# Attention stage of an audio tower: two of the six value slots multiplied ahead of the spreading of the maxima

## The reference, cut to what matters

```python
attn_grass = einsum('bhnd,bhmd->bhnm', qgr, kgr) ** 2 * grassman_scale   # qgr, kgr from QR
dots = einsum('bhnd,bhmd->bhnm', q, k)
a = concatenate([dots * scale, dots ** 2 * riem_scale, attn_grass], axis=1)
a = (a - bn_mean) * inv + bn_beta
a = einsum('oc,bcnm->bonm', conv_w, a) + conv_b
a = softmax(a, axis=-1)
out = einsum('bhnm,bhmd->bhnd', a, v)
```

## Time and profile before

| what | us |
|---|---|
| median of 3 runs (lowest to highest) | 908.42 (908.27 to 909.32) |
| the profiled execution's own time | 910.35 |
| span of the profiled execution | 908.7 |
| PE matmul busy | 798.0 (88%) |
| DVE busy | 719.1 (79%) |
| POOL busy | 506.5 (56%) |
| ACT busy | 439.6 (48%) |

### The profile page before, as it was taken

The page is one execution under the profiler, slowest core; times in us unless marked ns, Lnnn a source line. Parts: engine busy times, 40 slices in busy tenths (PEclk is TensorE's granted clock), DMA queues, the critical chain, the costliest instruction groups (busy, mean ns, idle before and its releaser), DMA issues. The chain is left out here.

```text
span 908.7 us, 39105 instructions
## 1 busy us (share of the span) xinstructions
PE 798.0 (88%) x16294; PEld 564.3 (62%) x16294; DVE 719.1 (79%) x1291; ACT 439.6 (48%) x902; POOL 506.5 (56%) x551
## 2 busy tenths in 40 slices
PE   3577857899896599999999999999999998799994
PEld 2233325555544477877778777777777776366663
DVE  4488895488798589999899998999998997376772
ACT  2233332211192165655555655555655555277773
POOL 3256571111000578888888888888888885122220
PEclk9578887799998599999999999999999999599998
DMA  8767200022330122222221122222222220001111
GB/s 289 273 212 248 84 1 0 9 54 54 81 88 1 53 70 62 63 62 67 76 63 62 62 65 72 69 62 63 62 64 76 66 62 22 1 18 29 29 28 33
DMA packets 64289, 64.85 MB, mean 71 GB/s; under 512 B 36825, under 2 KB 54812, under 8 KB 64156
## 3 DMA queue, kind: packets, MB, share of 16 engines
q1 hardware_dynamic: 63628, 61.24, 21.8%
q10 hardware_dynamic: 528, 1.54, 0.5%
HBM read 52.93 MB, written 6.75 MB: 66 GB/s over the span
## 5 line engine op out<-in xcount | busy, mean ns | idle before, releaser
L1169 ACT ACTIVATE sq<-ps_dot 128x376 f32<-128x376 f32 x384 | 165.0, 482 | 148.4 <-PE ps_dot L1066 148.4
L1066 PE MATMUL ps_dot<-q_st,k_blk 64*64 64x94 f32 x6144 | 170.5, 249 | 1.0 <-ACT sq L1169 0.8
L1066 PEld LDWEIGHTS ps_dot<-q_st,k_blk 64*64 64x64 f32 x6144 | 134.6, 134 | 46.5 <-issue 28.8
L999 POOL TENSOR_TENSOR v_blk<-v_rep,vmask 128x384 f32<-128x384 f32 x128 | 106.6, 853 | 12.9 <-PE ps_m L1096 7.3
L1014 POOL TENSOR_TENSOR half<-prob 128x564 f32<-128x564 f32 x64 | 75.5, 1180 | 60.5 <-ACT prob L1164 60.5
L1021 POOL TENSOR_TENSOR k_blk<-k_cm,hmask 128x768 f32<-128x768 f32 x64 | 96.8, 1513 | 1.1 <-PE ps_a L1108 1.1
L1023 POOL TENSOR_TENSOR k_mix<-k_cm,cols 128x768 f32<-128x768 f32 x64 | 96.8, 1513 | 0.0
L1192 DVE TENSOR_REDUCE row_max<-ps_a 128x94 f32<-128x564 f32 x128 | 88.8, 736 | 3.6 <-PE ps_a L1116 3.5
L367 PE MATMUL ps_spread<-parts,pair_sel 128*128 128x376 bf16 x256 | 58.1, 369 | 34.5 <-DVE prod L477 22.8
L1116 PE MATMUL ps_a<-sq,mix_w 64*32 64x282 f32 x2048 | 82.6, 404 | 0.3 <-ACT sq L1169 0.3
L1161 ACT ACTIVATE prob<-prob,head_const 128x564 f32<-128x564 f32 x64 | 49.1, 768 | 67.0 <-DVE prob L1214 67.0
(11 more groups left out here) (228 smaller groups left out, 1525.3 us busy)
## 6 DMA issues: line engine op xcount, KB each, us to landing
v_rep<-v_rows SPq DMA_DIRECT2D x128, 192.0 KB, 3.0
x_g<-in_x_dram SPq DMA_DIRECT2D x15, 1500.0 KB, 6.6
v_rows<-tok SPq DMA_DIRECT2D x16, 192.0 KB
q_st<-q_cm SPq DMA_DIRECT2D x64, 47.0 KB, 1.8
out_dram<-rows SPq DMA_DIRECT2D x16, 188.0 KB
x_g<-in_x_dram ACTq DMA_DIRECT2D x1, 1500.0 KB, 7.7
top_rows<-tok SPq DMA_DIRECT2D x16, 32.0 KB
top<-top_rows SPq DMA_DIRECT2D x1, 512.0 KB, 3.4
```

The costliest lines, as they stand in the source:

```text
L999: vb = pool.tensor_tensor(v_blk[:, a, b].rearrange("p t (o d) -> p (t o) d", o=H), v_rep[:, a, b].rearrange("p (t o d) -> p (t o) d", o=H, ...
L1066: mm = pe.matmul(ps_dot[64 * v:64 * v + 64, (2 * g + b) % 3, N * c:N * c + N], k_blk[rows, a, SLOTS * (3 * v + g) + c].rearrange("p k h m ...
L1169: act.activation(sq[:, b, :, g, :], ps_dot[:, (2 * g + b) % 3, 0:SLOTS * N].rearrange("p (c n) -> p c n", c=SLOTS), ACT.Square).then_inc(s ...
```

## The change

`attended` takes the slots that it is to do. Its three waits stand ahead of slot 0 only. In the steps from 2 on, slots 0 and 1 (8 of the 24 matmuls of the trace) are issued between `dots(i, a, 1)` and `spread_max(i - 1)`; slots 2 to 5 follow `spread_max` as before. The last two pairs, done after the loop, keep all six slots together. No other engine's list changes, and no operation is added or removed.

```diff
-            def attended(j, a):
-                pe.wait_ge(s["exp_done"], 2 * j + 2)
-                pe.wait_ge(s["v_ready"], j + 1)
-                if j:
-                    pe.wait_ge(s["out_done"], j)
-                for t in range(NT):
+            def attended(j, a, slots):
+                if 0 in slots:
+                    pe.wait_ge(s["exp_done"], 2 * j + 2)
+                    pe.wait_ge(s["v_ready"], j + 1)
+                    if j:
+                        pe.wait_ge(s["out_done"], j)
+                for t in slots:
                     for b in range(2):
                         pe.matmul(ps_m[64 * b:64 * b + 64, AV_AT:AV_AT + N], v_blk[:, a, b, t, :], prob[:, a, b, t, :],
                                   start=(t == 0), stop=(t == NT - 1), skip_group_check=True)
...
                 dots(i, a, 1)
+                if i >= 2:
+                    attended(i - 2, a, range(0, 2))
                 if i >= 1:
                     spread_max(i - 1)
                 if i >= 2:
-                    attended(i - 2, a)
+                    attended(i - 2, a, range(2, NT))
                     denominators(i - 2)
...
             for j in (PAIRS - 2, PAIRS - 1):
-                attended(j, j % 2)
+                attended(j, j % 2, range(NT))
                 denominators(j)
```

## The result

The changed kernel has a median of 913.64 us (912.64 to 915.21, 5 runs) against 908.42 (907.67 to 910.6, 5 runs): a ratio of 1.0053, 95% interval 1.0035 to 1.0071. It is slower by 5.2 us (3.2 to 6.5 by the interval); 5.1 were forecast.

The account below looks back on a forecast made before the run. VectorE with its 0.41 us round trip was taken as the bound, TensorE's idle time as slack. 60 steps at 0.085 us give 5.1, plus 0.1, minus 0.1: +5.1 on 908.42, so 913.5 us; range 910.0 to 917.0.

Parts of the forecast that it names:

- round trip on the transposes: VectorE's wait at line 1204 while TensorE transposes the second maxima: 0.41 us per step.
- The lateness of 0.25: Spreading's first load (line 1079) moves from 575.78 to 576.03, by 0.12 hole, 0.36 loads, 0.11 to 0.12 hole.
- The room of 0.16: `shift` (line 1210) could begin at 576.20 but begins at 576.36, held by the sums; the spreading may slip 0.16 us.
- 0.085: Forecast cost in us per step, paid in 60 steps: 0.12 + 0.36 + 0.11 - 0.34 - 0.16.
- The two ends: About 0.1 us added for the last two steps; 0.1 us won where TensorE had held VectorE up at line 1204.
- The narrow meeting: Second half of `linear` needs the last `sub_done` at 578.35 and starts loads at 578.41: it holds, narrowly.
- an idle time of 0.1 ahead of `shift`: Sign of a right prediction: line 1210 waits about 0.1 for line 1079 in 60 steps, 5 to 6 us together.
- line 1210 without idle time: Sign of a wrong prediction: `shift` on VectorE shows no wait after the change.
- the first rival: No hole between values and spreading: spreading 0.08 late, within the 0.16 us room, 908.3 us; chance 0.09.
- the second: TensorE is the bound, so only its own sum counts, 0.08 less per step x 62: 903.4 us; chance 0.04.
- the third: Costlier hole or no room: 923.4 us if all 0.25 shows, 934 with a 0.46 hole; chance 0.07.
- lateness less room: Spreading's 0.25 us delay less the 0.16 before `shift` is held up: `shift` begins 0.09 late in each step.

Follow-up runs that it names:

- keys_between: Kernel before with `turn_keys` moved between the second dots and the spreading, no value products there: 909.49 us, ratio 0.9999.
- sums_split: Kernel before with VectorE's sums (line 1224) cut in two, the first half moved ahead of line 1204: 903.86 us, ratio 0.9945 to before.
- one_slot: Changed kernel with one slot (4 of 24 value matmuls) ahead of the spreading instead of two: 907.83 us, ratio 0.9986 to before.
- three slots: Changed kernel with 12 value matmuls ahead of the spreading instead of 8: 924.20 us, ratio 1.0173 to before.
- sums_split_two: sums_split with the change on top (two slots ahead of the spreading): 914.16 us, ratio 1.0069 to the kernel before.
- sums_first_two: Changed kernel (two slots ahead) with VectorE's whole sums also moved ahead of line 1204: 913.51 us, ratio 1.0051 to the kernel before.

## Why the prediction was right

**The bound.** VectorE with its round trip on the transposes was the loop. Shown by keys_between (TensorE's stall filled, nothing gained) and by sums_split (an instruction of VectorE's moved into its 0.41 us wait, 5.7 us gained).

**The lateness of 0.25.** Holes of 0.11 (576.20 + 0.69 to 577.00) and 0.12, and 0.36 for the loads: the spreading stands 1.17 behind line 1207 instead of 0.92. The direction from 128x64 to 94x128 tiles, which the trace of before didn't have, costs what the way back does. The Trainium skill, TensorEngine Tiling (Array Packing), Tiling Modes, has any change of mode drain the array; the trace agrees in both directions, with 0.11 to 0.12 us here.

**The room of 0.16.** one_slot uses 0.09 of it and is not slower; two slots are 0.10 slower per step. With three, the spreading stands 1.33 behind line 1207 and `shift` 1.75, 0.41 and 0.25 later than before: once more 0.16 is absorbed. That puts the edge where the rows had it.

**The size.** 0.097 us per step was measured for 0.085. On the mean of the 59 steps the spreading's loads begin 0.250 later behind the first reduction over heads and `shift` 0.092, so that the lateness and the room were both sized rightly. What the sum lacked is the duration of `shift`: 414 ns instead of 400. It is 400 to 402 in the three kernels where `shift` goes on behind the sums (before, one_slot, keys_between) and 413 to 414 in the nine where the spreading releases it; why is not shown. The two ends that I had added and taken off, +0.1 and -0.1, were +0.04 in the last two steps and some -0.01 in each step of the loop. In all 5.7 us in 59 steps, for 5.1 in 60. That the medians give 5.2, a tenth from the forecast, is luck: their interval is 3.2 to 6.5 us, and the kernel before alone had medians from 908.4 to 909.5 in its four groups of runs.

**What would show it.** The period (7.19 and 7.29 in turn), line 1079's missing wait and the hole came as written, and TensorE's wait ahead of line 1073 rose to 0.30 on the mean, 0.35 in the step shown (0.3 forecast). The narrow meeting held: `linear` has no idle time after the change, and 5.2 us in 56 steps with three slots, where the lateness is larger. One sign was wrong: an idle time of 0.1 ahead of `shift` with line 1079 as its releaser. There are 0.7 us in 58 steps and no releaser, and "line 1210 without idle time" was even named as a sign of a wrong prediction. Its own rows spoke against that sign: they end the sums at 576.45 (575.65 + 0.80) and start the late `shift` at 576.45. `shift` used to begin 0.71 behind the start of the sums, 0.09 before their end; now it is 0.80 (577.10 to 577.90). The lateness was eaten out of an overlap of two rows, and a list of waits doesn't show that; only start-to-start distances do. With three slots the wait appears.

**The rivals.** The hole between products and spreading exists (the first rival). TensorE isn't the bound (the second): three slots would have been faster than two. The room is real (the third), by one_slot.

**What the prediction lacked** is that the cost has two regimes, set by the longer of two ways from the maxima to `shift`. It was right for the kernel as it stood, and my expectations for sums_split_two and sums_first_two, built on the same "lateness less room", missed the cost by 5 and 4 us.

## What to carry to other kernels

A stall on a busy engine is filled safely with work that ends before its releaser comes, or later by no more than the room that the next instruction of the bound engine has, and the change of tile shape on either side of the filler belongs to the filler's price. Before filling, compare the two ways to the next instruction of the engine that is the bound: the one over the releaser, and the one over the queue in which the filler stands; one slot stayed below that point and two went beyond it. If the engine that waits isn't the bound, fill the hole of the one that is. In this kernel half of the sums in VectorE's 0.41 us wait brought more than any filling of TensorE's 0.34 that was tried on the kernel before.

## What was not expected of the hardware

Most VectorE instructions in a row overlap by some 0.08 us in the trace (line 1206 and the sums, the sums and `shift`, the two of line 1192); `row_max_e` behind `row_max_o` is one that doesn't, with 0.03 between them. An instruction that its semaphore releases just as the one ahead ends loses that overlap without showing idle time (sums to `shift` 0.71 to 0.80 us from start to start) and takes 414 ns instead of 400. The hole at a change of TensorE's tile shape is the same 0.11 to 0.12 us whichever way it goes between 64x64, 128x64 and the whole array, with matmuls of 94 to 128 columns; after the mixing's 282 columns 0.45 to 0.46 stand there.
